# The idle rows' sums beside the down product instead of beside the key blocks, with three W2 places

## The chip, the cores and the metric

The program runs on one core of a Trainium2 chip. The metric is the device time of one execution in microseconds (us), the median of several runs; less is better. TensorE is PE in the profile, VectorE DVE, ScalarE ACT, GpSimd POOL and SyncE SP (SP only issues DMAs here).

## The reference, cut to what matters

A network of four parts over 32 x 128 = 4096 tokens of 256 numbers:

```
x = x + cross_attention0(layernorm(x), ctx, mask)        # 16 heads
x = x + feed_forward0(layernorm(x), gate, up, down)      # weights and activations quantised
x = x + cross_attention1(layernorm(x), ctx)              # 16 heads of 64, own output layernorm
for i in range(8):                                       # experts, on z = layernorm(x)
    mask = (argmax(z @ Wr + br) == i)
    h = relu((z * mask) @ W1[i] + b1[i])                 # 256 -> 1024
    out = out + (h @ W2[i] + b2[i])                      # 1024 -> 256
x = x + out
```

A token that is not expert i's still adds relu(b1[i]) @ W2[i] + b2[i]. These "idle rows" are one row of 256 numbers for each of the 8 experts, the same for all tokens. To compute them all of W2 has to be read (8 x 1024 x 256 float32, 8 MB).

## The kernel before, in words

Each part is a function with its own SBUF places and one block of code per engine; engines meet only through semaphores, and each engine goes through its list in order. The change is in `feed_forward0` (lines 640 to 1500 or so) and in one place of `experts`.

`feed_forward0` computes the feed-forward part and, between its own steps, the keys and values of `attention1`. From 444 us on its stages are:

1. **Key and value blocks.** PE computes 128 blocks (`key_block`, L1043, then `value_block`, L1053), 64 for keys and 64 for values, of 6 matmuls with 512 columns each. They go through 7 PSUM banks in turn. ACT copies each block from its bank into one of 5 buffers `outs` (`copy_block`, L1173 and L1175), SP stores it (L853, L858). `bank_free(n)` lets PE start block n once block n - 7 is copied. POOL loads the contexts, 1 MB for every 8 blocks, as earlier blocks finish (L905), and the value weights at the step from keys to values (L902).
2. Between the copies, in ACT's list, stands the feed-forward part's elementwise work: 12 units of `sigmoid` (two passes, L1157 and L1159) with 4 block copies behind each, then 3 copies, then 12 units of `quantise_silu` (L1164) with 3 or 4 copies each. DVE does `silu`, `times_up` and the maxima that the scales need; each scale waits for the last unit of its stage. After block 120 PE turns the down weights, and the last 8 blocks follow.
3. **The down product.** 32 tiles of 128 tokens, 18 matmuls with 256 columns each (`down`, L1089). ACT and DVE prepare `inner` for 4 tiles at a time; DVE adds the residual (`residual`, L1429); SP loads x1 and stores x2, 4 places each. On PE and SP all but the first turns stand in a hardware loop.

The idle rows: 16 pieces of W2, each 4 experts x 128 rows x 256 columns (512 KB in four DMAs, `load_w2`, L846), and for each piece 4 matmuls of 32 columns of weights each (`idle_sums`, L1018; the trace shows 8 records for them), added up in PSUM bank 7. Before the change they stand in stage 1, one behind every third block, from block 2 to block 47. There is a single W2 place in `x_space`: the load of piece i waits for the sums of piece i - 1 and stands in SP's list between the stores of blocks. `copy_idle` on ACT (L1183) stands behind the last sigmoid unit, and SP stores the rows (L882) in stage 3 of its list, at block 64.

At its start `experts` counts tokens and places them (DVE), spreads the idle rows over all partitions by 16 matmuls on PE (L2344), which ACT copies out (`other`, L2573), and multiplies `at_tile` and `at_row` (L2352) to find each slot's token number. ACT makes half of `at_tile` (L2577) after it has copied `other`. After that the tiles' gathers start.

```python
for n in range(ALL):
    ...
    if n % IDLE_EVERY == IDLE_EVERY - 1 and piece < 2 * FB:
        if piece == 0:
            pe.wait_ge(relu_b1_ready, 1)
        idle_sums(piece)
        piece += 1
```

Of the kernel before, what the change touches and what calls it, by code (L numbers as in the profile page):

```python
# [637 lines left out]
def feed_forward0(nc, ident, yT, ymax, upT, gateT, downT, w_gate, w_down, x1_dram, x2_dram, mv2, rstd2, b1T_dram, w2_dram,  # L638
# [16 lines left out]
    with ExitStack() as stack:  # L655
# [50 lines left out]
        w2 = x_space[:, 0:4 * D].rearrange("p (e d) -> p e d", d=D)  # L706
        idle = x_space[:, 0:BANK].rearrange("p (g d) -> p g d", g=2)
        down_int = x_space[:, BANK:BANK + NF * D // 4].bitcast(I16)
# [47 lines left out]
        w2_loaded = sem("w2_loaded")  # L756
# [40 lines left out]
        IDLE_EVERY = 3  # L797
# [14 lines left out]
        with nc.Block() as block:  # L812

            @block.sync
            def _(sp):
                def step(t, s):
                    if inside(t, 4, NB - 1):
                        sp.wait_ge(x2_ready, t - 3)
                    sp.dma_start(x1_sb[:, s, :], x1_dram[t]).then_inc(x1_loaded[s], 16)
                    if inside(t, 3, NB - 1):  # L820
                        store(t - 3, (s + 1) % 4)

# [18 lines left out]
                def load_w2(i):  # L841
                    g, f = divmod(i, FB)
                    if i >= 1:
                        sp.wait_ge(idle_part, i)
                    for e in range(4):
                        sp.dma_start(w2[:, e, :], w2_dram[4 * g + e][:, f, :]).then_inc(w2_loaded, 16)  # L846
# [24 lines left out]
                sp.wait_ge(product_done, 2 * NC * NF)  # L871
                load_w2(0)
                w2_pieces = 1
                for n in range(ALL):
                    store_block(n)
                    if n % IDLE_EVERY == IDLE_EVERY - 1 and w2_pieces < 2 * FB:
                        load_w2(w2_pieces)
                        w2_pieces += 1
                    if n == KEYS:
                        sp.wait_ge(idle_ready, 1)  # L880
                        for e in range(4):
                            sp.dma_start(idle_dram[e:NE:4].unsqueeze(0), idle[32 * e:32 * e + 1]).then_inc(idle_stored, 16)  # L882
                sp.wait_ge(block_done, ALL)
                sp.dma_start(wq_raw[:], wq_dram).then_inc(wq_loaded, 16)
                sp.wait_ge(idle_stored, 64)
                for n in range(NO):
                    sp.wait_ge(block_stored[n], 16 * ((ALL + NO - 1 - n) // NO))
                for t in range(4):
                    step(t, t)
                with sp.Fori(1, NB // 4) as i:  # L890
                    for s in range(4):
                        step(4 * i + s, s)
                for t in range(NB - 3, NB):
                    store(t, t % 4)
                sp.wait_ge(wq_loaded, 16)
                for s in range(4):
                    sp.wait_ge(x2_stored[s], 16 * NB // 4)
# [57 lines left out]
            def _(pe):  # L955
# [58 lines left out]
                def idle_sums(i):  # L1014
                    g, f = divmod(i, FB)
                    pe.wait_ge(w2_loaded, 64 * (i + 1))
                    for e in range(4):
                        last = pe.matmul(ps[32 * e:32 * (e + 1), 7, g * D:(g + 1) * D],  # L1018
                                         b1T[:, 4 * g + e, f:f + 1].to_broadcast([P, 32]), w2[:, e, :],
                                         start=(f == 0), stop=(f == FB - 1))  # L1020
                    last.then_inc(idle_part, 1)
# [35 lines left out]
                piece = 0  # L1057
                for n in range(ALL):
# [11 lines left out]
                    if n % IDLE_EVERY == IDLE_EVERY - 1 and piece < 2 * FB:  # L1070
                        if piece == 0:
                            pe.wait_ge(relu_b1_ready, 1)
                        idle_sums(piece)
                        piece += 1
# [3 lines left out]
                def down(c, s):  # L1078
                    first = isinstance(c, int) and c == 0
                    if not first:  # L1080
                        pe.wait_ge(inner_ready, c + TILES)
                    for t in range(TILES):
# [3 lines left out]
                        if inside(n, TILES, NB):  # L1086
                            pe.wait_ge(x2_ready, n - TILES + 1)
# [3 lines left out]
                        last.then_inc(down_done, 1)  # L1091

                for c in range(2):
                    down(c, c)
                with pe.Fori(1, NC // 2) as i:
                    for s in range(2):
                        down(2 * i + s, s)

            @block.scalar
            def _(act):  # L1100
# [80 lines left out]
                def copy_idle():  # L1181
                    act.wait_ge(idle_part, 2 * FB)
# [10 lines left out]
                copy_idle()  # L1193
# [890 lines left out]
def experts(nc, ident, logits, idle_dram, w, zx_dram, out):  # L2084
# [6 lines left out]
    with ExitStack() as stack:  # L2091
# [136 lines left out]
        with nc.Block() as block:  # L2228
# [310 lines left out]
            def _(act):  # L2539
# [28 lines left out]

                act.wait_ge(summed, 1)
# [112 lines left out]
```

## Time and profile before

| | us |
|---|---|
| median of 3 runs | 1651.63 (1647.52 to 1653.64) |
| the profiled execution's own time | 1649.6 |
| its span | 1647.8 |
| PE busy over the span | 1389.3 (84%) |
| DVE, ACT, POOL busy | 1183.1, 1047.2, 431.9 |
| key and value blocks on PE | 444.0 to 700.7 |
| down product, to the start of `attention1` | 703.9 to 774.7, 780.9 |
| mean granted clock of PE | 0.92 of full speed |

The busy share of an engine is an average over stages. For one stage one asks which engine has no gap there, and where it has gaps, who ended them. The granted clock is 1.0 at 2.4 GHz and 0.5 at 1.2 GHz; a value between is a mixture over the stretch.

### The profile page before, as it was taken

The page shows a single profiled execution, that of the slowest core. Times are in us where ns is not written, and L with a number is a line of the kernel's source. Part 1 is how long each engine was busy: PE and PEld are TensorE (multiplying, and loading weights), DVE is VectorE, ACT ScalarE, POOL GpSimd, SP SyncE. Part 2 cuts the span into 40 slices and gives each one's busy share as a digit, 9 for nine tenths or more (in the row PEclk, how much of TensorE's full clock was granted, in tenths as well). Part 3 has the DMA queues.
Part 4 walks back from the last instruction along what each step waited for, and adds up shares of the span by engine and source line. Part 5 has one row for each costly group of instructions (what it writes and reads, how often), then busy time and mean ns, then how long its engine had stood idle before and what let it go on. Part 6 is the DMA issues. An engine that isn't in the chain of part 4 may idle for free. (4 is left out here: it accounts for less than half of the span.)

```text
span 1647.8 us, 35334 instructions
## 1 busy us (share of the span) xinstructions
PE 1389.3 (84%) x11229; PEld 1184.0 (72%) x11229; DVE 1183.1 (72%) x2102; ACT 1047.2 (64%) x2716; POOL 431.9 (26%) x735
## 2 busy tenths in 40 slices
PE   5788888898867689998788888898888867999997
PEld 3455555686744468898677778787777757999996
DVE  6688777887645569086477777777777766888885
ACT  4677778574466656463566666666666625888885
POOL 5444443000000001002123222323232313444443
PEclk9999999899988889999799989989998878999998
DMA  7311010472366778743413232232323135511110
GB/s 225 100 31 35 29 35 28 144 280 90 113 195 199 231 240 268 261 139 109 169 65 114 93 103 77 83 121 76 102 76 120 38 129 210 195 45 54 54 47 9
DMA packets 106773, 194.91 MB, mean 118 GB/s; under 512 B 13474, under 2 KB 72893, under 8 KB 100288
## 3 DMA queue, kind: packets, MB, share of 16 engines
q1 hardware_dynamic: 96320, 160.13, 29.0%
q0 software_dynamic: 10176, 33.57, 6.8%
q8 instruction: 47, 0.77, 0.2%
q14 instruction: 38, 0.31, 0.1%
q10 hardware_dynamic: 192, 0.13, 0.0%
HBM read 128.49 MB, written 68.03 MB: 119 GB/s over the span
## 5 line engine op out<-in xcount | busy, mean ns | idle before, releaser
L1996 ACT ACTIVATE c_w_raw<-c_ps_score,c_shift 128x128 f32<-128x128 f32 x512 | 184.0, 393 | 172.3 <-DVE c_shift L1872 135.9
L2373 PE MATMUL d_ps_hT<-d_zT,d_w_tile 128*128 128x128 f32 x1248 | 148.5, 278 | 1.6 <-DVE d_zT L2480 1.6
L2373 PEld LDWEIGHTS d_ps_hT<-d_zT,d_w_tile 128*128 128x128 f32 x1248 | 145.3, 195 | 2.3 <-DVE d_zT L2480 2.3
L2386 PE MATMUL d_ps_y<-d_w_parts,d_hT 128*128 128x256 f32 x936 | 121.8, 287 | 1.8 <-DVE d_res L2511 1.8
L1996 ACT ACTIVATION_READ_ACCUMULATOR c_w_raw<-c_ps_score,c_shift 128x1 f32 x512 | 118.8, 232 | 0.0
L2386 PEld LDWEIGHTS d_ps_y<-d_w_parts,d_hT 128*128 128x128 f32 x936 | 114.6, 191 | 2.0 <-DVE d_res L2511 2.0
L581 ACT ACTIVATE a_probT<-a_ps_probT 128x512 f32<-128x512 f32 x128 | 71.1, 623 | 66.2 <-PE a_ps_probT L368 66.2
L459 DVE TENSOR_REDUCE a_row_max<-a_ps_score 128x8 f32<-128x1024 f32 x64 | 78.0, 1218 | 48.6 <-PE a_ps_score L357 48.6
L2546 ACT ACTIVATE d_h<-d_ps_hT,d_b1T 128x128 f32<-128x128 f32 x312 | 88.7, 367 | 37.8 <-PE d_ps_hT L2373 37.8
L2499 DVE TENSOR_TENSOR d_w_parts<-d_w,d_w_parts 128x1024 fp32r<-128x1024 f32 x78 | 95.2, 1221 | 23.7 <-ACT d_w_parts L2558 23.7
L1754 PE MATMUL c_ps_proj<-c_xnT,c_wq 128*128 128x256 f32 x768 | 105.9, 288 | 0.0
L1801 PE MATMUL c_ps_aux<-c_wo,c_attnT 128*128 128x256 f32 x768 | 99.3, 285 | 3.0 <-DVE c_attnT L1892 2.9
L1724 PE MATMUL c_ps_score<-c_kT,c_qT 64*128 64x128 f32 x1024 | 92.6, 332 | 8.5 <-ACT c_w_raw L1996 6.9
L1754 PEld LDWEIGHTS c_ps_proj<-c_xnT,c_wq 128*128 128x128 f32 x768 | 94.4, 191 | 3.8 <-issue 0.2
L1801 PEld LDWEIGHTS c_ps_aux<-c_wo,c_attnT 128*128 128x128 f32 x768 | 93.6, 191 | 4.8 <-issue 3.4
L1724 PEld LDWEIGHTS c_ps_score<-c_kT,c_qT 64*128 64x128 f32 x1024 | 79.2, 232 | 24.8 <-ACT c_w_raw L1996 12.7
L1869 DVE TENSOR_REDUCE c_row_max<-c_ps_score 128x4 f32<-128x512 f32 x128 | 87.4, 683 | 7.7 <-PE c_ps_score L1724 7.5
L1699 POOL TENSOR_TENSOR c_var_o<-c_mv_o,c_eps 128x1 f32<-128x1 f32 x32 | 6.8, 213 | 327.0 <-DVE c_mv_o L1915 327.0
L1878 DVE RECIPROCAL c_inv_sum<-c_row_sum 128x4 f32<-128x4 f32 x128 | 22.4, 175 | 97.1 <-ACT c_w_raw L1996 97.1
L1880 DVE TENSOR_TENSOR c_w_raw<-c_w_raw,c_inv_sum 128x512 f32<-128x512 f32 x128 | 88.6, 692 | 4.5 <-DVE c_inv_sum L1878 0.2
L1043 PE MATMUL b_ps<-b_ctx_high,b_w_parts 128*128 128x512 f32 x256 | 91.9, 431 | 0.0
L2558 ACT ACTIVATE d_w_parts<-d_w 128x1024 fp32r x78 | 80.4, 1054 | 13.7 <-PE d_ps_y L2386 12.6
(299 smaller groups left out, 3731.3 us busy)
## 6 DMA issues: line engine op xcount, KB each, us to landing
keys_scratch<-b_out SPq DMA_DIRECT2D x64, 256.0 KB, 3.6
values_scratch<-b_out SPq DMA_DIRECT2D x64, 256.0 KB, 3.6
c_kT<-keys_scratch SPq DMA_DIRECT2D x16, 1024.0 KB, 6.4
d_w<-w_in SPq DMA_DIRECT2D x16, 1024.0 KB, 8.0
split_scratch<-b_split SPq DMA_DIRECT2D x12, 1024.0 KB, 4.7
c_v_more<-values_scratch SPq DMA_DIRECT2D x24, 512.0 KB, 3.9
b_ctx_high<-split_scratch POOLq DMA_DIRECT2D x16, 512.0 KB, 6.1
b_ctx_low<-split_scratch POOLq DMA_DIRECT2D x16, 512.0 KB, 7.5
```

Source lines behind the costliest of these rows:

```text
L1043: last = pe.matmul(ps[:, bank(n), :], w_parts[:, h, a, k, column:column + P], ctx_parts[c % 2][b][:, k, :], start=(j == 0), stop=(j == ND ...
L1724: last = pe.matmul(ps_score[:, r, j, :], qT[rows, s, blk, tok], kT[rows, s, blk, tok], start=True, stop=True)
L1754: last = pe.matmul(ps_proj[:, j, h * PT:(h + 1) * PT], weights[:, a, k, blk * P:(blk + 1) * P], src[:, c, k, :], start=(n == 0), stop=(n = ...
L1801: last = pe.matmul(ps_aux[:, 0:D], attnT[:, s, a, blk, :], wo[:, c, blk, :], start=(n == 0), stop=(n == BLKS * len(PARTS) - 1))
L1869: dve.tensor_reduce(row_max[:, n, :], ps_score[:, n % 2], AX_X, ALU.max).then_inc(max_done, 1)
L1880: dve.tensor_tensor(prob[:, n], prob[:, n], inv_sum[:, n, :].unsqueeze(2).to_broadcast([P, HB, P]), ALU.mult).then_inc(prob_ready, 1)
L1996: last = act.activation(prob[:, n, j, :], ps_score[:, n % 2, j, :], ACT.Exp, scale=float(KD) ** -0.5, bias=shift[:, n, j:j + 1], accum_out ...
L2373: last = pe.matmul(ps_hT[:, f, :], w1_tile[:, half, k, n * P:(n + 1) * P], zT[:, s, k, :], start=(k == 0), stop=(k == ND - 1))
L2386: last = pe.matmul(ps_y[:, 0:D], hT[:, s, a, f, :], w2_parts[:, half, b, n, :], start=(f == 0 and (a, b) == PARTS[0]), stop=(f == FB - 1 a ...
L2499: dve.tensor_tensor(w2_parts[:, half, 1], w2[:, e, half * FB // 2:(half + 1) * FB // 2, :], w2_parts[:, half, 0].bitcast(F32), ALU.subtrac ...
L2546: act.activation(h[:, f, :], ps_hT[:, f, :], ACT.Relu, bias=b1T[:, e, f:f + 1]).then_inc(h_ready, 1)
L2558: act.activation(w2_parts[:, half, 0], w2[:, e, half * FB // 2:(half + 1) * FB // 2, :], ACT.Copy)\
```

## The change

The sums move from the blocks' loop into the down product: one piece behind every second tile, 16 pieces for 32 tiles. The W2 pieces lie in three places in turn, where the contexts lay before (`yT`, `upT`, `gateT`), so piece i waits for the sums of piece i - 3. The loads stand in SP's list behind every second x1 load. The two hardware loops of the down product on PE and SP become straight code. The idle rows go through `out2`; ACT copies them behind its last `high_inner`, and SP stores them ahead of the last x2 tile. In `experts` ACT makes its half of `at_tile` ahead of the copies of `other`.

```diff
-        w2 = x_space[:, 0:4 * D].rearrange("p (e d) -> p e d", d=D)
-        idle = x_space[:, 0:BANK].rearrange("p (g d) -> p g d", g=2)
-        down_int = x_space[:, BANK:BANK + NF * D // 4].bitcast(I16)
+        w2 = [raw_at(f"w2_{n}", [P, 4, D], offset)
+              for n, offset in enumerate((address["yT"] + 4 * (2 * T - ITEM), address["upT"], address["gateT"]))]
+        idle = out2[:].rearrange("p (g d) -> p g d", g=2)
+        down_int = x_space[:, 0:NF * D // 4].bitcast(I16)
...
@@ sync: step, load_w2 and the list @@
                     sp.dma_start(x1_sb[:, s, :], x1_dram[t]).then_inc(x1_loaded[s], 16)
-                    if inside(t, 3, NB - 1):
+                    if t >= 3:
                         store(t - 3, (s + 1) % 4)
+                    if t % 2 == 0:
+                        load_w2(t // 2)
...
-                    if i >= 1:
-                        sp.wait_ge(idle_part, i)
+                    if i >= 3:
+                        sp.wait_ge(idle_part, i - 2)
                     for e in range(4):
-                        sp.dma_start(w2[:, e, :], w2_dram[4 * g + e][:, f, :]).then_inc(w2_loaded, 16)
+                        sp.dma_start(w2[i % 3][:, e, :], w2_dram[4 * g + e][:, f, :]).then_inc(w2_loaded[i % 3], 16)
...
-                sp.wait_ge(product_done, 2 * NC * NF)
-                load_w2(0)
-                w2_pieces = 1
                 for n in range(ALL):
                     store_block(n)
-                    if n % IDLE_EVERY == IDLE_EVERY - 1 and w2_pieces < 2 * FB:
-                        load_w2(w2_pieces)
-                        w2_pieces += 1
-                    if n == KEYS:
-                        sp.wait_ge(idle_ready, 1)
-                        for e in range(4):
-                            sp.dma_start(idle_dram[e:NE:4].unsqueeze(0), idle[32 * e:32 * e + 1]).then_inc(idle_stored, 16)
...
-                for t in range(4):
-                    step(t, t)
-                with sp.Fori(1, NB // 4) as i:
-                    for s in range(4):
-                        step(4 * i + s, s)
-                for t in range(NB - 3, NB):
-                    store(t, t % 4)
+                for t in range(NB):
+                    step(t, t % 4)
+                store(NB - 3, (NB - 3) % 4)
+                store(NB - 2, (NB - 2) % 4)
+                sp.wait_ge(idle_ready, 1)
+                for e in range(4):
+                    sp.dma_start(idle_dram[e:NE:4].unsqueeze(0), idle[32 * e:32 * e + 1]).then_inc(idle_stored, 16)
+                store(NB - 1, (NB - 1) % 4)
                 sp.wait_ge(wq_loaded, 16)
+                sp.wait_ge(idle_stored, 64)
@@ tensor: the blocks' loop loses the sums (quoted above), down gets them @@
                         last.then_inc(down_done, 1)
+                        if n == 1:
+                            pe.wait_ge(relu_b1_ready, 1)
+                        if n % 2 == 1:
+                            idle_sums(n // 2)
...
-                for c in range(2):
-                    down(c, c)
-                with pe.Fori(1, NC // 2) as i:
-                    for s in range(2):
-                        down(2 * i + s, s)
+                for c in range(NC):
+                    down(c, c % 2)
@@ scalar: copy_idle moves from behind the last sigmoid unit to the end @@
-                copy_idle()
                 copy_blocks(done, done + 3)
...
                         high_inner(2 * i + s, s)
+                copy_idle()
@@ vector and tensor: two waits on the idle rows go @@
-                        dve.wait_ge(idle_stored, 64)
-                        pe.wait_ge(idle_ready, 1)
@@ experts, scalar @@
+                act.wait_ge(consts, 11)
+                act.wait_ge(hot_ready, 1)
+                act.activation(at_tile[:, :, 0], in_tile_hot[:], ACT.Copy, scale=token_no[:]).then_inc(tokens_ready, 1)
                 act.wait_ge(summed, 1)
                 ...
-                act.wait_ge(consts, 11)
-                act.wait_ge(hot_ready, 1)
-                act.activation(at_tile[:, :, 0], in_tile_hot[:], ACT.Copy, scale=token_no[:]).then_inc(tokens_ready, 1)
```

## Rows read from the trace of the kernel before

**Rows 1.** Busy time by stretch; columns: stretch, its us, busy us (instructions) per engine, clock, DMA share, GB/s.
```profile
444.00:586.20 142.20, 98.85 (x446) 68.51 (x445) 72.32 (x49) 80.76 (x78) 9.55 (x16) 0.83 0.68 204
...
607.00:700.70 93.70, 93.61 (x396) 75.64 (x396) 49.51 (x38) 54.76 (x77) 6.74 (x13) 0.97 0.81 275
700.70:774.70 74.00, 70.80 (x576) 70.63 (x576) 58.48 (x106) 39.48 (x18) 8.70 (x4) 0.98 0.42 133
774.70:780.90 6.20, 0.01 (x1) 0.00 (x0) 1.29 (x6) 0.00 (x1) 1.28 (x3) 0.69 0.06 21
```
**Rows 2.** Waits from 443 to 607 us; columns: who waits, for whom, total us, times, longest.
```profile
ACT b_out L1173 <- PE b_ps L1043: 62.0, 30, 7.7
...
PE b_ps L1018 <- DMA b_x_space<-w_in: 43.4, 10, 8.6
```
**Rows 3.** Timeline, PE between 444 and 481 us; columns: start, us, engine, line, what, [idle before].
```profile
445.40 0.62 PE L1043 MATMUL b_ps<-b_ctx_high,b_w_parts 128*128 128x512 f32 x2
...
446.09 0.62 PE L1043 MATMUL b_ps<-b_ctx_high,b_w_parts 128*128 128x512 f32 x2
...
472.96 1.08 PE L1018 MATMUL b_ps<-b_x_space,b_b1T 128*32 128x256 f32 x8 [8.60 <-DMA b_x_space<-w_in]
...
479.25 0.39 PE L1043 MATMUL b_ps<-b_ctx_high,b_w_parts 128*128 128x512 f32 x1
479.56 0.64 PE L1018 MATMUL b_ps<-b_x_space,b_b1T 128*32 128x256 f32 x8
480.13 0.50 PE L1043 MATMUL b_ps<-b_ctx_high,b_w_parts 128*128 128x512 f32 x1
```
**Rows 4.** Timeline, ACT from the first sigmoid to the third.
```profile
457.42 1.28 ACT L1157 ACT_TABLE_LOAD   x1
...
462.57 2.40 ACT L1173 ACTIVATE b_out<-b_ps,b_bk 128x512 f32<-128x512 f32 x4
...
468.71 0.67 ACT L1173 ACTIVATE b_out<-b_ps,b_bk 128x512 f32<-128x512 f32 x1
```
**Rows 5.** Timeline, ACT and DVE around the step from silu to the up product.
```profile
572.02 1.91 ACT L1159 ACTIVATE b_act<-b_act 128x2048 int32<-128x2048 f32 x1
...
580.08 0.16 DVE L1265 TENSOR_TENSOR b_factors<-b_one 128x1 f32<-128x1 f32 x1
...
590.33 3.89 ACT L1164 ACTIVATE yT<-b_act,b_factors 128x2048 int16<-128x2048 f32 x2
```
**Rows 6.** Timeline, POOL and PE around the step from key blocks to value blocks.
```profile
596.97 0.55 POOL L902 DMA_DIRECT2D b_w_parts<-split_scratch  x1 [17.56 <-PE b_ps L1043]
...
607.03 1.22 PE L1053 MATMUL b_ps<-b_w_parts,b_ctx_high 128*128 128x512 f32 x2 [4.76 <-DMA b_ctx_low<-split_scratch]
```
**Rows 7.** Waits from 607 to 704 us, one row.
```profile
ACT b_out L1175 <- DMA values_scratch<-b_out: 8.2, 7, 1.5
```
**Rows 8.** Timeline, SP: the first x1 loads.
```profile
703.76 1.76 SPq L819 DMA_DIRECT2D b_x_space<-x_scratch  x4
```
**Rows 9.** The loads of W2 at line 846: time from issue to landing.
```profile
DMA to landing us min/median/max: 2.2/2.7/7.8
```
**Rows 10.** Timeline, SP and POOL: the idle rows' stores, and the end of this part.
```profile
611.38 2.54 SPq L882 DMA_DIRECT2D idle_scratch<-b_x_space  x4
...
769.13 6.46 SPq L825 DMA_DIRECT2D x_scratch<-b_x_space  x4
...
776.57 1.04 POOL L952 TENSOR_TENSOR rstd<-b_var,b_power 128x4 f32<-128x4 f32 x1
```
**Rows 11.** Timeline, start of the experts' part.
```profile
1356.31 4.62 DVE L2461 TENSOR_TENSOR d_at_row<-d_numbers,d_slot_row_f 128x1024 bf16<-128x1024 bf16 x4
...
1357.14 1.39 ACT L2577 ACTIVATE d_w_tile<-d_in_tile_hot,d_token_no 128x1248 bf16<-128x1248 bf16 x1
...
1360.99 0.70 PE L2352 MATMUL d_ps_ids<-d_w_tile,d_at_row 128*128 128x78 bf16 x8 [0.43 <-DVE d_at_row L2461]
...
1367.56 0.66 PE L2361 MATMUL d_ps_zT<-ident,d_zx 128*128 128x128 f32 x2 [5.88 <-DMA d_zx<-zx_scratch,d_zx_ids]
```

More of the change, by code:

```diff
@@ L755, in feed_forward0 @@
         relu_b1_ready = sem("relu_b1_ready")
-        w2_loaded = sem("w2_loaded")
+        w2_loaded = [sem(f"w2_loaded{n}") for n in range(3)]
         raw_loaded = [sem(f"raw_loaded{s}") for s in range(2)]
@@ L796, in feed_forward0 @@
         TURN_FROM = ALL - 8
-        IDLE_EVERY = 3
+        IDLE_PIECES = 2 * FB
         WK, CONTEXT, WV = 0, 2, 2 + NC
@@ L816, in step @@
                 def step(t, s):
-                    if inside(t, 4, NB - 1):
+                    if t >= 4:
                         sp.wait_ge(x2_ready, t - 3)
                     sp.dma_start(x1_sb[:, s, :], x1_dram[t]).then_inc(x1_loaded[s], 16)
-                    if inside(t, 3, NB - 1):
+                    if t >= 3:
                         store(t - 3, (s + 1) % 4)
+                    if t % 2 == 0:
+                        load_w2(t // 2)
                 def store(t, s):
@@ L870, in _ @@
                         load_raw(k + 2)
-                sp.wait_ge(product_done, 2 * NC * NF)
-                load_w2(0)
-                w2_pieces = 1
                 for n in range(ALL):
                     store_block(n)
-                    if n % IDLE_EVERY == IDLE_EVERY - 1 and w2_pieces < 2 * FB:
-                        load_w2(w2_pieces)
-                        w2_pieces += 1
-                    if n == KEYS:
-                        sp.wait_ge(idle_ready, 1)
-                        for e in range(4):
-                            sp.dma_start(idle_dram[e:NE:4].unsqueeze(0), idle[32 * e:32 * e + 1]).then_inc(idle_stored, 16)
                 sp.wait_ge(block_done, ALL)
                 sp.dma_start(wq_raw[:], wq_dram).then_inc(wq_loaded, 16)
-                sp.wait_ge(idle_stored, 64)
                 for n in range(NO):
                     sp.wait_ge(block_stored[n], 16 * ((ALL + NO - 1 - n) // NO))
-                for t in range(4):
-                    step(t, t)
-                with sp.Fori(1, NB // 4) as i:
-                    for s in range(4):
-                        step(4 * i + s, s)
-                for t in range(NB - 3, NB):
-                    store(t, t % 4)
+                for t in range(NB):
[6 more added lines that the diff above has]
+                store(NB - 1, (NB - 1) % 4)
                 sp.wait_ge(wq_loaded, 16)
+                sp.wait_ge(idle_stored, 64)
                 for s in range(4):
@@ L1015, in idle_sums @@
                     g, f = divmod(i, FB)
-                    pe.wait_ge(w2_loaded, 64 * (i + 1))
+                    pe.wait_ge(w2_loaded[i % 3], 64 * (i // 3 + 1))
                     for e in range(4):
                         last = pe.matmul(ps[32 * e:32 * (e + 1), 7, g * D:(g + 1) * D],
-                                         b1T[:, 4 * g + e, f:f + 1].to_broadcast([P, 32]), w2[:, e, :],
+                                         b1T[:, 4 * g + e, f:f + 1].to_broadcast([P, 32]), w2[i % 3][:, e, :],
                                          start=(f == 0), stop=(f == FB - 1))
@@ L1055, in value_block @@
                     last.then_inc(block_done, 1)
-                piece = 0
                 for n in range(ALL):
@@ L1069, in _ @@
                         value_block(n)
[L1070 to L1074, printed above, removed]
                 pe.wait_ge(block_copied, ALL)
@@ L1078, in down @@
                 def down(c, s):
-                    first = isinstance(c, int) and c == 0
+                    first = c == 0
                     if not first:
@@ L1085, in down @@
                             pe.wait_ge(inner_ready, t + 1)
-                        if inside(n, TILES, NB):
+                        if n >= TILES:
                             pe.wait_ge(x2_ready, n - TILES + 1)
@@ L1181, in copy_idle @@
                 def copy_idle():
-                    act.wait_ge(idle_part, 2 * FB)
+                    act.wait_ge(idle_part, IDLE_PIECES)
                     act.activation(idle, ps[:, 7, :].rearrange("p (g d) -> p g d", g=2), ACT.Copy).then_inc(idle_ready, 1)
```

## The prediction

> **What bounds the kernel now.** I read the page first for its span (1647.8 us), then busy time by stretch, then the waits of the stretch that the change empties, then single timelines. In 607 to 700.7 PE is busy 93.61 of 93.70 us: the 64 value blocks are bound by PE. The stretch 444 to 586.2, the key blocks with the idle sums among them, is another matter: PE is busy 98.85 of 142.2 us, its clock 0.83, and ACT, the next busiest, 80.76 [rows 1]. The waits say why: PE's sums wait 43.4 us in ten pieces for W2 loads, and ACT in turn waits 62.0 us for PE's blocks [rows 2]. So nobody is saturated there; one late DMA holds PE, PE holds ACT, and ACT holds the sigmoid chain. The down product (700.7 to 774.7) is again PE's, 70.80 busy of 74.00, with DMA at 0.42 [rows 1].
>
> What PE would need without the sums: three matmuls start every 0.69 us (445.40 to 446.09) [rows 3], 1.38 us a block. By 586.2 52 blocks are copied (4, and 4 behind each of 12 sigmoid units), 71.8 us of PE work. The other 142.2 - 71.8 = 70.4 us are the sums: 43.4 us of waits, 16 groups, and matmuls at the low clock after long waits (a group takes 1.01 us from 472.96 after a wait of 8.60, and 0.57 from 479.56 without one [rows 3]).
>
> **Part 1, the sums leave the blocks.** At most 70.4 us go. What is late next is ACT. Its cycle of one sigmoid unit and four copies, when nothing keeps it waiting, is 462.57 to 468.71, 6.14 us [rows 4]; I take 6.25 as PSUM and semaphores never fit so well throughout. PE needs 4 x 1.38 = 5.52 for the same four blocks, so it runs ahead until 7 banks are full. The first unit starts once the first four blocks are copied: 444.0 + 5.5 + 0.7 = 450.2, and 1.3 for the table load [rows 4], 451.5. Twelve cycles end at 451.5 + 75.0 = 526.5.
>
> Then the scale: from the last sigmoid pass (573.93) to the factor (580.24) 6.3 us pass, and two quantise units of 3.89 us follow before the next copy [rows 5]. The last pass ends 2.3 us before the cycle does, so the factor is there at 530.5 and the next copy at about 535. PE, 7 blocks ahead, has finished block 61 by 531 and stands for some 4 us. This stall is new, but it falls onto one that exists: the value weights and context 8 are loaded when block 59 is finished, and value block 64 starts 10.0 us after that issue (596.97 to 607.03) [rows 6]. Block 59 is finished at about 528.6, so value block 64 starts at 538.7 whether PE stood before or not. From there on I take the whole stretch of before, 93.6 us [rows 1]; it includes the restart of PE at the low clock. DVE and ACT are by then some two units less advanced against PE than before, but they are busy only 49.51 and 54.76 of these 93.70 us [rows 1], so their units still end ahead of PE's blocks. Blocks end at 538.7 + 93.6 = 632.3.
>
> Stores: without W2 the DMAs carry per 6.25 us four blocks (1 MB) and half a context (0.5 MB), 252 GB/s; the value stretch carried 275 at a share of 0.81 [rows 1]. Where ACT waited for stores there it was 8.2 us in 7 waits over 64 blocks [rows 7]. ACT is the bound of the key stretch, so such waits count: I add 3 us (between 0 and the 8.2). Blocks end at 635.3 instead of 700.7: **-65.4 us**. The bounds: -70.4 (all of it goes) and, from above, the key stretch at the DMA rate of before (rival 1), -41.
>
> **Part 2, the sums join the down product.** PE is full there, so each group is paid in full. In 479.25 to 480.13 a group between two matmuls takes 0.88 us where 0.23 is the usual spacing: 0.65 [rows 3]. 16 x 0.65 = **+10.4 us**. Bounds: 9.1 (16 x 0.57) and 16 x 1.3 = 21 with each group at the pace of the one at 472.96.
>
> Do they wait? A W2 piece needs four issues on SP, 0.44 us each as for x1 (1.76 for four) [rows 8], and lands 2.2 to 7.8 us after, median 2.7 [rows 9]. Piece i is issued when the residual of tile 2i - 3 is done and is used after tile 2i + 1. A tile takes 70.8 / 32 = 2.2 us [rows 1], plus half a group. DVE runs the residuals of four tiles together, behind its part of the next four, so in the worse turn the piece is issued about 8 us after the end of the earlier chunk and used about 15 after: 7 us for 1.8 of issuing and 2.7 of landing. The wait on the sums of piece i - 3 is long satisfied. Queued behind these four issues on SP are an x1 load and an x2 store; both have 4 places and three tiles (7 us) of room against 1.8. Piece 0 is the tight one: it is issued behind the 1 MB load of wq and the first x1 load, from 703.76 + 0.44 to about 706 [rows 8], and needed behind two tiles, at 703.9 + 4.4 and 1 or so for the restart at the low clock, 709.3: 3 us, about the median landing. 0 us, and 3 as the bound. I cost the straight code instead of the loops at nothing, hidden by PE's own matmuls: PE has no gap at a loop's turn now (70.80 busy of 70.8 between 703.9 and 774.7) [rows 1]; bounds -1 and +1.
>
> **Part 3, the tail.** Before, PE ends at 774.7, x2's last store is issued at 775.59, POOL ends at 777.61 [rows 10], and the next part starts at 780.9 [rows 1]. Now, after the last group: ACT's copy 0.6 and its signals 0.2, four small stores 2.54 (611.38) [rows 10], x2's last store 0.35, its landing 1.9 us: 5.6 us, in place of POOL's 2.9. **+2.7 us**; bounds 0 and 5. No other work lies beside it, as all engines meet at the block's end.
>
> **Part 4, the experts.** ACT's 1.39 us for `at_tile` would start at about 1355 instead of 1357.14. But the last 8 matmuls wait for DVE's `at_row`, which ends at 1360.94 in any case, and the first use of `other`, PE's turn at 1367.56, waits for a gather [rows 11]; 1.4 us later for `other` harms nobody. 0 us; bounds -0.5 and +0.5. The W2 traffic there doesn't change. The two waits on the idle rows that go (on DVE and PE) had been met long before.
>
> **Sum.** -65.4 + 10.4 + 2.7 = -52.3 us. The profiled execution's own time is 1649.6, so 1597.3; the median of the runs lies 2.0 above it: 1599 us.
>
> **The rivals.**
> 1. *The blocks become bound by DMA.* For it: W2 leaves, but the blocks come faster, and the key stores go in rows of 1 KB; the stretch of before moved 204 GB/s at a share of 0.68 [rows 1]. Against it: that share leaves room, and long PE waits leave DMA idle in it. If 204 GB/s were the limit, the 142.2 us x 204 = 29.0 MB less 8.4 MB of W2 would need 101 us: 41 us saved, not 65. Then 1599 + 24 = 1623.
> 2. *The loads of W2 come a little late in the down product too*, for they now share SP's list with x1 and x2. At 1.2 us a piece (half of a tile) it costs 19 us: 1618. Against it: the 7 us of room.
> 3. *The wait moves with the sums* (the other side). The largest landing was 7.8 us [rows 9], and a long wait also leaves PE at the low clock behind it. Were each piece so late that the whole 70.4 us of excess stood in the down product, the change would be 70.4 - 65.4 + 2.7 = +7.7: 1659. It decides from 3.3 us of loss a piece on ((65.4 - 10.4 - 2.7) / 16), in place of the 43.4 us of waits before, which were with one place, and with 512 KB in competition with stores and contexts at 204 GB/s, where the down product moves 133 [rows 1]. The Trainium skill, TensorE: Matmul & The Clock Gate, HAM oscillation, warns of just this: a matmul burst, a DMA wait, a burst again, each restarting at the low clock. That this trace agrees is seen at 472.96 [rows 3]; by that rule it turns on whether a wait comes at all.
> 4. *The change does not do what it says*: the sums weren't what held the key stretch, and ACT takes over at once. It holds it at 6.14 to 6.3 a cycle, as counted above; but now it waits 2.1 us on average each time that it waits for PE (62.0 in 30) [rows 2]; were one such wait left in every other cycle, 13 us less would be saved: 1612.
>
> **Chances.** Forecast 0.70 (own range 1589 to 1610: -70.4 and +9.1 at one end, 3 for piece 0, 5 in the tail and 5 more of store waits at the other), rival 1 0.10, rival 2 0.08, rival 3 0.03, rival 4 0.09. A range of 1588 to 1621 leaves out the larger half of rival 1, rival 3 and small tails. A difference below 0.5% (8 us) can't be told from none here. Only rival 3 is slower: slower 0.03, within 0.02, faster 0.95.
>
> **What would show it.** From 444 to the end of the value blocks 191 us instead of 256.7, with PE's clock near 1 in the key stretch, no wait of PE for `w_in` there, and ACT near full between 452 and 527 on the old clock; PE's wait in front of the first value block stays near 5 us. The down product takes 85 us instead of 74, its 128 rows of sums without idle time before them. From PE's last matmul to the next part 9 us instead of 6.2. The distance of the experts' start to the first gathered tile is unchanged. The prediction is wrong if ACT waits for `keys_scratch` more than some 8 us in total in the key stretch, or if PE shows waits for `w_in` over 3 us in the down product.

## The result

| | before | after |
|---|---|---|
| median of 4 runs each, us | 1649.72 (1647.52 to 1653.64) | 1593.75 (1592.08 to 1599.37) |
| the profiled execution's own time | 1649.6 | 1592.1 |
| its span | 1647.8 | 1590.3 |

The ratio is 0.966 (95% interval 0.963 to 0.970). The same kernel run twice more, beside the kernel before each time, gave 0.965 (0.962 to 0.968) and 0.966 (0.963 to 0.969). The prediction was 1599 us, in the range 1588 to 1621, and the median of 1593.75 lies in it. The profiled execution lost 57.5 us where 52.3 were forecast.

### The profile page after: what moved, and what is told of

Same layout as the page of the kernel before. It is cut to its first block and busy times, and to the rows that moved or that the text cites. A ratio compares the mean times of both kernels' runs of the same rounds, so it can differ in the third digit from the quotient of the medians.

```text
span 1590.3 us, 35168 instructions
## 1 busy us (share of the span) xinstructions
PE 1376.9 (87%) x11229; PEld 1179.9 (74%) x11229; DVE 1187.1 (75%) x2102; ACT 1043.0 (66%) x2716; POOL 439.8 (28%) x735
## 5 line engine op out<-in xcount | busy, mean ns | idle before, releaser
L1103 ACT ACTIVATE b_act<-b_ps 128x512 f32<-128x512 f32 (+1 forms) x96 | 54.8, 600 | 52.6 <-PE b_ps L988 45.3
```

## The profile after

First the busy time by stretch: the key stretch to the first value block, the value blocks, the down product to the end of the last sums, and the tail. Columns as in [rows 1].

```profile
443.67:541.97 98.30, 91.51 (x386) 71.38 (x385) 81.74 (x54) 89.17 (x89) 13.84 (x22) 1.00 0.78 248
541.97:634.35 92.38, 92.36 (x396) 74.72 (x396) 54.58 (x39) 57.85 (x80) 6.72 (x13) 0.98 0.87 289
634.35:720.36 86.01, 82.78 (x704) 73.97 (x704) 59.77 (x107) 39.50 (x18) 8.78 (x4) 0.98 0.70 213
720.36:725.97 5.61, 0.00 (x1) 0.00 (x0) 0.81 (x5) 0.60 (x1) 1.27 (x3) 0.73 0.07 25
```

The key stretch, where PE was busy 98.85 of 142.20 us at a clock of 0.83 [rows 1], is now 98.30 us long with PE busy 91.51 of them, clock 1.00, and ACT at 89.17. The down product is longer and moves 213 GB/s instead of 133. Set against the stages of before:

| stage | before | after | difference | forecast |
|---|---|---|---|---|
| start to first key matmul | 444.0 | 443.7 | -0.3 | 0 |
| key and value blocks | 256.6 | 190.7 | -65.9 | -65.4 |
| down product with its sums | 74.1 | 86.0 | +11.9 | +10.4 |
| to the next part's first issue | 6.2 | 5.6 | -0.6 | +2.7 |
| `attention1` and `experts` | 866.9 | 864.3 | -2.6 | 0 |
| span | 1647.8 | 1590.3 | -57.5 | -52.3 |

Next the waits from 443 to 607 us (who waits, for whom, total us, times, longest), which answer [rows 2]:

```profile
ACT b_out L1161 <- DMA keys_scratch<-b_out: 7.4, 4, 4.1
PE b_ps L1046 <- DMA b_ctx_low<-split_scratch: 4.0, 1, 4.0
ACT b_out L1161 <- PE b_ps L1036: 2.8, 4, 0.8
PE b_ps L1036 <- ACT b_out L1161: 2.7, 8, 0.4
```

ACT waits for PE 2.8 us instead of 62.0, and nobody waits for `w_in`. ACT's own list shows its new cycle:

```profile
450.33 1.28 ACT L1145 ACT_TABLE_LOAD   x1
...
455.48 2.41 ACT L1161 ACTIVATE b_out<-b_ps,b_bk 128x512 f32<-128x512 f32 x4
457.77 2.02 ACT L1145 ACTIVATE b_act<-yT,b_factors 128x2048 f32<-128x2048 int16 x1
459.81 1.92 ACT L1147 ACTIVATE b_act<-b_act 128x2048 int32<-128x2048 f32 x1
461.64 0.67 ACT L1161 ACTIVATE b_out<-b_ps,b_bk 128x512 f32<-128x512 f32 x1
...
474.75 2.40 ACT L1161 ACTIVATE b_out<-b_ps,b_bk 128x512 f32<-128x512 f32 x4
477.03 2.02 ACT L1145 ACTIVATE b_act<-yT,b_factors 128x2048 f32<-128x2048 int16 x1
479.08 1.92 ACT L1147 ACTIVATE b_act<-b_act 128x2048 int32<-128x2048 f32 x1
480.91 1.24 ACT L1161 ACTIVATE b_out<-b_ps,b_bk 128x512 f32<-128x512 f32 x2
```

455.48 to 461.64 and 474.75 to 480.91 are 6.16 us each: one unit of sigmoid and four copies without a gap. The step from keys to values, on PE and on the queue of POOL:

```profile
524.69 0.50 PE L1036 MATMUL b_ps<-b_ctx_high,b_w_parts 128*128 128x512 f32 x1 [0.36 <-ACT b_out L1161]
532.23 0.55 POOL L896 DMA_DIRECT2D b_w_parts<-split_scratch  x1 [2.68 <-PE b_ps L1036]
534.94 0.50 PE L1036 MATMUL b_ps<-b_ctx_high,b_w_parts 128*128 128x512 f32 x1 [0.21 <-ACT b_out L1161]
541.97 1.16 PE L1046 MATMUL b_ps<-b_w_parts,b_ctx_high 128*128 128x512 f32 x2 [3.97 <-DMA b_ctx_low<-split_scratch]
```

One group of sums between two tiles of the down product on PE, which answers [rows 3]:

```profile
704.27 0.28 PE L1076 MATMUL b_ps<-b_down_high,b_inner 128*128 128x256 f32 x1
704.48 0.64 PE L1011 MATMUL b_ps<-b_w,b_b1T 128*32 128x256 f32 x8
705.05 0.39 PE L1076 MATMUL b_ps<-b_down_high,b_inner 128*128 128x256 f32 x1
705.28 0.28 PE L1076 MATMUL b_ps<-b_down_low,b_inner 128*128 128x256 f32 x1
```

And the tail, the timeline of all engines, which answers [rows 10] (SPq is SP's queue of DMA issues):

```profile
719.72 0.64 PE L1011 MATMUL b_ps<-b_w,b_b1T 128*32 128x256 f32 x8
719.83 0.48 DVE L1416 SCALAR_TENSOR_TENSOR b_x_space<-b_ps,b_factors,b_x_space 128x256 f32<-128x256 f32 x1 [1.14 <-PE b_ps L1076]
720.43 0.60 ACT L1171 ACTIVATE b_out<-b_ps 128x512 f32<-128x512 f32 x1 [18.15 <-PE b_ps L1011]
721.05 2.54 SPq L886 DMA_DIRECT2D idle_scratch<-b_out  x4
721.66 1.04 POOL L946 TENSOR_TENSOR rstd<-b_var,b_power 128x4 f32<-128x4 f32 x1
723.64 0.40 SPq L828 DMA_DIRECT2D x_scratch<-b_x_space  x1
725.97 0.10 POOL L1661 MEMSET c_power<- 128x1 f32 x1 [3.27 <-POOLq L813]
```

## The experiments

Theory: the wait for W2 in the blocks' list held PE, PE held ACT; without it ACT bounds the key stretch; in the down product only the matmuls of the sums are paid, since the loads have room. Rivals: one of the other edits (straight loops, order in `experts`) carries a part; three places, not the position, made the difference; DMA traffic is paid somewhere. The stage times in us, each from one profile (blocks; down product up to its last own matmul, so without the group behind that; from there to `attention1`'s first transpose of `c_xn`; from that to the first work of `experts`; `experts`):

| kernel | blocks | down | tail | attention1 | experts | time, us |
|---|---|---|---|---|---|---|
| before | 255.9 | 74.2 | 8.9 | 561.4 | 303.1 | 1649.72 (4 runs) |
| order_only | 254.1 | 74.2 | 9.1 | 563.7 | 300.7 | 1651.43 (12) |
| straight_only | 260.8 | 74.1 | 9.1 | 560.6 | 302.2 | 1652.39 (12) |
| blocks_loads_earlier | 232.8 | 74.2 | 9.0 | 561.1 | 303.6 | 1624.58 (4) |
| tail_no_pow | 259.5 | 74.3 | 8.0 | 562.6 | 302.6 | 1652.18 (1) |
| after | 190.0 | 85.6 | 9.0 | 561.9 | 299.9 | 1593.75 (4) |
| after_again | 190.1 | 85.5 | 9.0 | 561.9 | 300.9 | 1592.6 (6) |
| after_third | 190.9 | 85.6 | 9.0 | 560.9 | 302.1 | 1594.7 (6) |
| down_without_w2 | 189.8 | 74.2 | 9.0 | 560.3 | 302.1 | 1582.91 (4) |
| down_loads_only | 190.2 | 74.2 | 11.3 | 564.0 | 303.4 | 1587.66 (4) |
| down_one_place | 191.0 | 89.7 | 9.4 | 558.5 | 302.6 | 1596.55 (4) |
| context8_early | 190.6 | 85.8 | 9.0 | 561.3 | 301.2 | 1593.76 (6) |
| pairs | 191.4 | 82.4 | 9.4 | 562.3 | 299.6 | 1590.68 (6) |
| half_rounding | 186.2 | 87.0 | 9.0 | 561.1 | 299.7 | 1591.41 (1) |

Without a pattern the two right-hand stages move by some 5 and 4 us. The blocks of the four kernels that leave them as in before move from 254.1 to 260.8, and PE's waits for W2 there move with them: 41.1 us in order_only, 43.4 in before, 44.2 in tail_no_pow, 46.6 in straight_only.

**order_only**: the kernel before, with ACT's half of `at_tile` ahead of the copies of `other`.

```diff
+                act.wait_ge(consts, 11)
+                act.wait_ge(hot_ready, 1)
+                act.activation(at_tile[:, :, 0], in_tile_hot[:], ACT.Copy, scale=token_no[:]).then_inc(tokens_ready, 1)
                 act.wait_ge(summed, 1)
...
-                act.wait_ge(consts, 11)
-                act.wait_ge(hot_ready, 1)
-                act.activation(at_tile[:, :, 0], in_tile_hot[:], ACT.Copy, scale=token_no[:]).then_inc(tokens_ready, 1)
```

> The kernel before with only the experts' edit: ScalarE makes its half of at_tile ahead of the copies of the idle rows. Theory (the gain is the key stretch's): nothing, within 1 us, as the last eight id matmuls start when VectorE's at_row ends (1360.94 before) and the first gathered tile is turned some 22.8 us after the experts' start in both. Rival (the experts' part, which ran 3.1 us shorter in the changed kernel, does so because of this edit): 3 us less, some 1646 against 1649.

Ratio to before 1.001 (0.998 to 1.003). The distance from `experts`' start to the first gathered tile is 22.9 us as before. No gain shows. The interval reaches some 4 us to either side, more than the 2.6 us that `attention1` and `experts` gave in the first profile of after, so the total alone would not rule them out; that they are not this edit's work is read from the distance, which has not moved.

**straight_only**: the kernel before, with the down product's loops on PE and SP written out.

```diff
-                with sp.Fori(1, NB // 4) as i:
-                    for s in range(4):
-                        step(4 * i + s, s)
+                for t in range(NB):
+                    step(t, t % 4)
...
+                for c in range(NC):
+                    down(c, c % 2)
```

> The kernel before with only the hardware loops of the down product on TensorE and SyncE written out. Theory: nothing, within 1 us; the 576 down matmuls stay at 70.8 us. Rival (the 1.5 us that the down product of the changed kernel takes beyond 16 groups of 0.65 come from straight code): 1.5 us more, seen as TensorE gaps between 703.9 and its last matmul.

0.999 (0.997 to 1.001), and the down product takes 74.1 us where it took 74.2: no gain and no loss shows.

**down_without_w2**: the kernel after, without the loads of W2 and without the sums; the idle rows are left out of the result.

```diff
-                    if t % 2 == 0:
-                        load_w2(t // 2)
...
-                        if n == 1:
-                            pe.wait_ge(relu_b1_ready, 1)
-                        if n % 2 == 1:
-                            idle_sums(n // 2)
...
-                    act.wait_ge(idle_part, IDLE_PIECES)
+                    act.wait_ge(down_done, NB)
```

> The changed kernel with neither the 64 loads of W2 nor the sums (the idle rows are left out, what is stored in their place is whatever the PSUM bank holds). Theory: the down product loses the 16 groups, 10.5 to 12 us, the block stretch stays at 190.7 us; 1582 against 1594. Rival (sums in the down product are hidden by its waits, or W2's loads disturb more than the sums cost): under 5 us, or well over 12 us.

0.958 (0.954 to 0.962). The down product falls to 74.2, what it was before; the 15 groups ahead of its last matmul cost 11.4 us, 0.76 each. In the total it is 10.8 (1593.75 - 1582.91).

**down_loads_only**: the loads stay, the matmuls of the sums go (the idle rows are left out of the result); a place is loaded again when its load before has landed.

```diff
                     if i >= 3:
-                        sp.wait_ge(idle_part, i - 2)
+                        sp.wait_ge(w2_loaded[i % 3], 64 * (i // 3))
```

> The changed kernel with the loads of W2 in the down product and without the sums' matmuls (idle rows left out as in the other). Theory: the loads cost nothing; the time is that of the kernel without both, 1582, within 1 us. Rival (SyncE's list holds x1 and x2 up behind four W2 issues): part of the 12 us stays, with TensorE waiting for x2_ready or VectorE for x1.

0.960 (0.956 to 0.964). 8 MB more of loads leave the down product at 74.2 us: PE's matmuls lose nothing by them, so the 11.4 us are PE's own. But the total is 4.7 us above down_without_w2, not within 1 us as expected; the intervals against before overlap, yet three of the four runs are longer than all four of down_without_w2. 2.3 us of it stand in the tail, and the trace names them (waits from 635 to 712 us, then SP's issues ahead of the last residual, which starts at 711.89):

```profile
DVE b_x_space L1414 <- DMA b_x_space<-x_scratch: 7.7, 7, 2.0
```

```profile
706.54 1.91 SPq L849 DMA_DIRECT2D b_w<-w_in  x4
708.49 0.43 SPq L820 DMA_DIRECT2D b_x_space<-x_scratch  x1
```

The last x1 load stands behind the last W2 load in SP's list, and DVE waits 1.98 us for it. This is the expectation's rival, in part: the W2 issues hold an x1 load up in SP's list. In after there is no such wait, since the product lasts 11.4 us longer and the last x1 load is issued at 714.47, 5 us ahead of its use. The rest of the 4.7 lies in the stages that scatter and stays open.

**after_again** and **after_third** are the kernel after unchanged; they show the scatter and stand beside the others on the same chips.

> The changed kernel as it is, on the chip of the other runs of this call, so that they can be compared with it. 1594 against 1651.

> The changed kernel once more, beside the next one on the same chip. 1593.

Both reproduce the result; `experts` took 299.9, 300.9 and 302.1 us in the three profiles of one and the same kernel.

**down_one_place**: the kernel after with a single W2 place; the load of piece i waits for the sums of piece i - 1.

```diff
-                    if i >= 3:
-                        sp.wait_ge(idle_part, i - 2)
+                    if i >= 1:
+                        sp.wait_ge(idle_part, i)
...
-                        sp.dma_start(w2[i % 3][:, e, :], w2_dram[4 * g + e][:, f, :]).then_inc(w2_loaded[i % 3], 16)
+                        sp.dma_start(w2[0][:, e, :], w2_dram[4 * g + e][:, f, :]).then_inc(w2_loaded[0], 16)
```

> The changed kernel with one W2 place instead of three: each load waits for the sums of the piece before it. Theory (what matters is that the sums are behind every second tile, 5.1 us apart, against 1.9 us of issuing and 2.7 of landing): waits of 0 to 1 us a piece, at most 10 us in all, 1594 to 1604. Rival (three places are what makes it work; with one the waits of the blocks come back, some 3 us a piece and the low clock behind them): 40 us or more, 1635 and up.

0.968 (0.964 to 0.972); the down product takes 89.7 instead of 85.6. Its waits there:

```profile
DVE b_x_space L1416 <- DMA b_x_space<-x_scratch: 12.3, 8, 2.2
PEld b_ps L1011 <- DMA b_w<-w_in: 5.7, 9, 1.9
PE b_ps L1011 <- DMA b_w<-w_in: 3.7, 5, 1.7
```

The waits come back, and the x1 loads, which share SP's list, are waited for too, but 4.1 us is 0.26 a piece, against 43.4 us in all with one place in the blocks [rows 2]. The position carried nearly the whole gain; the three places are worth 4 us of the down product in the profiles (in the total, 1596.55 against 1592.6, the intervals overlap).

**blocks_loads_earlier**: the kernel before, each W2 load two blocks further ahead in SP's list.

```diff
-                    if n % IDLE_EVERY == IDLE_EVERY - 1 and w2_pieces < 2 * FB:
+                    while w2_pieces < 2 * FB and n == max(0, IDLE_EVERY * w2_pieces - 4):
```

> The kernel before, with the sums where they were and one W2 place, but each W2 load two blocks earlier in SyncE's list (behind the store of block 3k - 4 instead of 3k - 1). In the list a load stands behind the store of a block that ScalarE copies late, after its sigmoid passes. Theory (the wait is the list's: TensorE is ahead of ScalarE's copies, so the load is issued too late): over half of the 43.4 us of waits go, 1605 to 1625. Rival (the wait is DMA's rate in the key stretch, or the single place): under 10 us, 1640 and up.

0.984 (0.980 to 0.988): 23 us of the blocks' 256 go, with one place and the old position. Its waits from 443 to 607 us:

```profile
ACT b_out L1173 <- DMA keys_scratch<-b_out: 26.1, 11, 4.3
PE b_ps L1018 <- DMA b_x_space<-w_in: 23.2, 7, 4.3
```

PE's waits for W2 fall from 43.4 to 23.2. So about half of them was not the transfer but the list: the load stood behind stores that were waiting for ACT's copies, and ACT was waiting for PE. The trace of before shows it at the third piece. The sums of the second piece, which free the place, end at 460.0, but SP's list reaches the load only here, behind three stores whose blocks ACT was late to copy:

```profile
457.42 6.79 SPq L853 DMA_DIRECT2D keys_scratch<-b_out  x3
464.26 2.58 SPq L846 DMA_DIRECT2D b_x_space<-w_in  x4
```

PE stands from 464.36 until the piece is there at 472.96 [rows 3], some 6 us behind the last of the four issues, where the median landing is 2.7 [rows 9]. So this load was late by its place in the list and slow besides; why it was slow no run here separates. In exchange ACT now waits 26.1 us for its stores: one list feeds both, and one of them is late.

**context8_early**: the kernel after, with context 8 issued on POOL ahead of the maximum and the value weights. This was the wait of 3.97 us ahead of the first value block.

```diff
-                load_contexts(2, 8)
+                load_contexts(2, 9)
                 maximum(SILU)
...
-                load_contexts(8, 9)
```

> The changed kernel, with context 8 loaded ahead of the SILU maximum and of the first half of the value weights, as soon as block 55 is finished. Theory: TensorE waits 4.0 us for it at the step from keys to values and then runs some 6 us at the low clock; both go or shrink, 4 to 7 us less, 1589. Rival (the wait belongs to the DMA rate at that point, 3 MB in 10 us, and only changes its name, to the value weights or to ScalarE's key stores): under 2 us.

0.965 (0.962 to 0.968), blocks 190.6: no gain. From 520 to 640 us ACT waits 22.1 us for the stores of the values, where it waits 8.6 in after:

```profile
ACT b_out L1162 <- DMA values_scratch<-b_out: 22.1, 9, 4.6
```

PE's wait for the context is gone, and the first value block starts 2.1 us sooner, counted from the first key block. But PE now waits for ACT's copies at the value blocks, which it did not do in after:

```profile
PE b_ps L1045 <- ACT b_out L1160: 3.4, 2, 1.9
```

Not all of ACT's 22.1 us count, for ACT's waits for PE's value blocks fell from 19.6 to 6.2 in exchange. The step is bound by several things at once, as the expectation's rival said.

**half_rounding**: the kernel after, with ACT's second sigmoid pass over half of its columns (the rounding of the other half is left out).

```diff
-                    act.activation(unit.bitcast(I32), unit, ACT.Copy, scale=65536.0).then_inc(sig_rounded, 1)
+                    act.activation(unit[:, 0:UNIT // 2].bitcast(I32), unit[:, 0:UNIT // 2], ACT.Copy, scale=65536.0).then_inc(sig_rounded, 1)
```

> The changed kernel with ScalarE's second sigmoid pass (times 65536, to integer) over half of the columns only; the other half is left unrounded, so the sigmoid's values are wrong. Theory (ScalarE bounds the key stretch, with VectorE's 5.86 us a unit right behind its 6.15): units come every 5.9 us instead of 6.15, TensorE waits less for copies, and the stage from the first to the twelfth unit is 2 to 4 us shorter. Rival (DMA bounds the stretch at its 245 GB/s): no change in the distance of the units.

The first sigmoid passes of after (duration in ns, minimum, median, maximum, then first and last start in us):

```profile
L1145 ACT ACTIVATE b_act<-yT,b_factors x12: 2000/2020/2027, 451.6 to 520.1; 128x2048 f32<-128x2048 int16 x12
```

and of half_rounding:

```profile
L1145 ACT ACTIVATE b_act<-yT,b_factors x12: 2000/2018/2023, 454.4 to 518.5; 128x2048 f32<-128x2048 int16 x12
```

Busy time in the stretch from 451.6 to 525 us, columns as in [rows 1], of after:

```profile
451.60:525.00 73.40, 70.79 (x299) 55.20 (x298) 63.22 (x33) 72.54 (x71) 8.88 (x12) 1.00 0.78 247
```

and of half_rounding, with its wait for stores in about the same stretch (450 to 527) below:

```profile
451.60:525.00 73.40, 73.40 (x320) 59.61 (x319) 65.37 (x35) 67.30 (x77) 7.26 (x12) 1.00 0.84 269
```

```profile
ACT b_out L1161 <- DMA keys_scratch<-b_out: 4.7, 4, 1.5
```

The unit's mean distance falls from (520.1 - 451.6) / 11 = 6.23 us to (518.5 - 454.4) / 11 = 5.83, and the blocks from 190 or 191 to 186.2. A shorter ACT pass shortens the stretch: ACT is its bound in after. It isn't by much: the pass shrinks by 0.86 us (1.92 to 1.06), of which 0.40 arrives; PE is at once busy the whole time, and ACT's waits for stores grow from 0.4 to 4.7 us. The down product's 87.0 instead of 85.6 is one wait of PE for W2, 1.35 us at 654.09. This is one profile and one run; the total, 1591.41, shows nothing by itself.

**pairs**: the kernel after with two pieces of sums behind every fourth tile.

```diff
-                        if n == 1:
+                        if n == 3:
                             pe.wait_ge(relu_b1_ready, 1)
-                        if n % 2 == 1:
+                        if n % 4 == 3:
+                            idle_sums(n // 2 - 1)
                             idle_sums(n // 2)
```

> The changed kernel with two pieces of sums behind every fourth tile in place of one behind every second. Theory (of a group's 0.77 us, 0.31 is the gap ahead of its first matmul and 0.11 the slower restart behind it, paid for each switch between 128-column and 32-column weights): 8 switches less, 3 to 4 us off the down product, 1590; the last pair lies behind the last tile and may give 0.6 us back in the tail. Rival (the time is the matmuls' own): no change of the down product, 1593.

0.964 (0.961 to 0.967). A pair on PE:

```profile
654.51 0.28 PE L1076 MATMUL b_ps<-b_down_high,b_inner 128*128 128x256 f32 x1
654.72 1.07 PE L1011 MATMUL b_ps<-b_w,b_b1T 128*32 128x256 f32 x16
655.72 0.39 PE L1076 MATMUL b_ps<-b_down_high,b_inner 128*128 128x256 f32 x1
```

The down product falls to 82.4. A pair costs (82.4 - 74.2) / 7 = 1.17 us where two single groups cost 1.52: 0.35 us is paid once for each time that PE leaves the down product for sums and comes back, however many pieces lie between. The runs don't tell what in this switch costs it, for the sums differ from the down matmuls in several ways at once: 32 columns of weights instead of 128, another bank, and plain float32 operands. The profile gives 2.8 us less for the product and its tail (85.6 + 9.0 against 82.4 + 9.4); the total's interval overlaps that of after, so it isn't shown to be the faster kernel.

**tail_no_pow**: the kernel before, GpSimd's last power turned into a multiplication (the last four tiles' normalisation factors are left out).

```diff
+                    if n < 2:
                         pool.tensor_tensor(rstd2[:, part], var2[:, part], power[:, part], ALU.pow).then_inc(rstd_done, 1)
+                    else:
+                        pool.tensor_tensor(rstd2[:, part], var2[:, part], power[:, part], ALU.mult).then_inc(rstd_done, 1)
```

> The kernel before, with GpSimd's last power of the down product's tail (rstd of the last four tiles) made a multiplication, so that these values are wrong. Theory (the start of the next part hangs on GpSimd's last instruction, which takes some 3 us beyond its recorded 1.04, and so hid SyncE's four idle stores in the changed kernel): the distance from TensorE's last down matmul to the next part's first transpose falls from 9.0 us by 1 to 3 us, to where x2's last store lands. Rival (the 3.3 us are the blocks' common end and follow whatever comes last): it falls by under 0.5 us.

The timeline of its tail has these two lines of POOL:

```profile
779.29 0.20 POOL L955 TENSOR_TENSOR rstd<-b_var,b_power 128x4 f32<-128x4 f32 x1
782.77 0.10 POOL L1677 MEMSET c_power<- 128x1 f32 x1 [3.27 <-POOLq L812]
```

The instruction shrank by 0.84 us (1.04 to 0.20) and the tail by about as much (8.9 to 8.0). The next part starts 779.49 to 782.77 = 3.28 us behind POOL's last instruction, as in before (777.61 to 780.88, 3.27) and in after (722.70 to 725.97, 3.27). The start of the next part hangs on POOL's chain, and no other chain stood within these 0.84 us. The fall, some 0.9 us, lies between the theory (1 to 3) and its rival (under 0.5): the start does follow POOL's last instruction, but the 3.27 us are no part of the power, since they stay behind the multiplication.

## Why the prediction was right, and where it was not

**What bounded the kernel: right.** One late DMA held PE, and PE held ACT. Without the sums PE's clock in the key stretch is 1.00, and ACT's waits for PE fall from 62.0 us to 2.8. What the prediction did not say is why the load was late; blocks_loads_earlier shows that about half of it was its place in SP's list, a loop over four engines (store waits for copy, copy for block, block for sums, sums for the load behind the store).

**Part 1, the blocks: -65.9 for -65.4, with errors inside that cancel.** ACT takes over at 6.16 us a unit (6.23 on average with its few waits; 6.25 assumed), and half_rounding shows that it is the bound, by little. The step to the values was reasoned wrongly in one place. PE was to finish block 59 at 528.6 and the first value block to start 94.7 us after the first key block; it started after 98.3. PE's lead of 7 blocks counts from the start of a burst of copies, not from its end, so PE finished block 59 only about 532, when POOL issued the value weights (532.23); PE's stall for copies behind it was 0.21 us, not 4. The wait behind the issue itself, 532.23 to 541.97, was 9.7 us for the 10.0 read from [rows 6]. Against these +3.6 us stand the value stretch (92.4 for 93.6) and the 3 us added for stores: from 450 to 527 us ACT waited 0.4 for them, and 6.9 of its 7.4 lay behind that, beside the wait for the value weights and context 8. That the sum came out within 0.5 us is luck beyond that too: over the profiles of kernels with the blocks of before these take 254.1 to 260.8 us, so the difference could as well have been 64 or 70.

**Part 2, the down product: +11.9 for +10.4, the mis-sized term.** A group costs 0.77 us, not 0.65. I measured from the matmul ahead to the first one behind (0.88 less 0.23 in [rows 3]). In after that is 704.27 to 705.05 less 0.12, 0.66; but the second matmul behind comes 0.23 later where 0.12 is usual, 0.11 more. The rows of before show it as well: 480.13 to the next start at 480.47 is 0.34 instead of 0.23. One row further would have given 0.76. The rest of the part held: no engine waits for W2 in after, whose issues (L849) show the time to their landing,

```profile
DMA to landing us min/median/max: 2.3/2.8/3.6
```

and neither the loads (down_loads_only) nor the straight code (straight_only) lengthen PE's stretch. What the loads can cost stands in SP's list: the 2.3 us in the tail of down_loads_only.

**Part 3, the tail: -0.6 for +2.7, the step that failed.** The prediction put SP's chain of 5.6 us in the place of POOL's 2.9 and kept the 3.3 us that came behind POOL. The chain's length was right: from the end of the last sums to the next part are 5.61 us. What failed is the path: the 3.27 us come behind POOL's last instruction and not behind SP's last store (tail_no_pow, pairs), so SP's chain runs beside them. Its last store is issued by 724.04, 1.9 us ahead of the start at 725.97, and the idle rows' copy and four stores fit into time that was already lost. They only just fit. In pairs, where SP's chain comes later against POOL's, the next part starts 2.25 us behind the start of the last store's issue (717.95 to 720.20); in after it is 2.33 us (723.64 to 725.97). By these two, an estimate, SP's chain had less than 0.1 us to spare. And POOL's own chain starts from the last tile, beside the last group of sums (DVE at 719.83, the sums at 719.72), so the sixteenth group costs nothing: 11.9 - 0.6 = 11.3 is 15 groups of 0.76.

**Part 4, the experts: right, 0** (order_only). The 2.6 us less in `attention1` and `experts` are scatter between executions: over the profiles of this case the first takes 558.5 to 564.0 us and the second 299.6 to 303.6, whichever kernel it was. Of the 5.2 us by which the profiled execution fell below its forecast (57.5 less 52.3), the tail makes 3.3, these 2.6, the blocks and their start 0.8, and the groups take 1.5 back.

**The rivals.** 1 (bound by DMA at 204 GB/s) fell: the same stretch moved 248 GB/s, half_rounding 269 and the value blocks 289. It has a grain of truth: stores begin to be waited for as soon as ACT gets shorter or a context comes early. 2 and 3 (the loads late in the down product) fell: PE has no wait for W2 in the three profiles of after, one of 1.4 us in half_rounding and two of 1.6 us together in context8_early; the longest landing was 3.6 us, and even with one place a piece costs 0.26 us, far from the 3.3 from which rival 3 would decide. The warning of the Trainium skill that the prediction cites at rival 3 (TensorE: Matmul & The Clock Gate, HAM oscillation) had nothing to act on: in after no wait of PE for W2 came between the tiles, and the clock of the product is 0.98 as before. 4 (ACT doesn't take over at once) fell: 2.8 us of waits for PE are left of 62.0, and 0.7 of them in the stretch from 450 to 527.

## What to carry to other kernels

A load that shares an in-order list with stores can be late because of what stands ahead of it, whatever the transfer takes; before moving its consumer, look at which engine the head of that list waits for, and give the pair a stage where the list doesn't wait on the same engine. Price work that is put into a full engine from the last undisturbed instruction ahead of it to the second one behind it. At a stage's end find out which engine's last instruction starts the next stage; work of the others beside its wait is free as long as it ends sooner.

## What the hardware showed beyond that

- Between a part's last instruction on GpSimd and the first of the next part lie 3.27 us in 13 of the 14 profiles. What fills them no run here shows. In pairs, where SP's last store came later against POOL, the gap was 3.62, and the start came 2.25 us behind that store's issue.
- Leaving the down matmuls for a group of sums and coming back costs PE about 0.35 us a round trip beyond the sums themselves, by the single and the doubled group. Which difference between the two kinds of matmul costs it isn't shown.
- In the down product the DMAs went from 133 to 213 GB/s beside PE, and the same loads without the sums left its matmuls at 74.2 us (down_loads_only); the late x1 load there added 2.3 us behind them.
